# Attention and expert layer: tile 3 transposed in its own step, values behind the next scores, ScalarE and VectorE copies rearranged

## What is computed

```
h  = layernorm(x)
k, v = split((h @ w_kv_down) @ w_kv_up)         # 16 heads of 64
q  = h @ w_q
y  = softmax(causal(q k^T / 8)) v
x  = x + y @ w_out
h  = layernorm(x)
combine = softmax of the top 2 of (h @ Wr), 8 experts
x  = x + sum_e combine_e * 12**-0.5 * (silu(h @ Wg_e) * (h @ Wu_e)) @ Wd_e
```

## Time and profile before

| | |
|---|---|
| median of 3 runs | 951.95 us (951.78 to 955.58) |
| profiled execution | 954.19 us, its span 952.4 us |
| attention steps 1 to 62 | 32.2 to 685.3 us of the span |
| first expert tile | 732.3 us |
| busy over the span | TensorE 94%, VectorE 65%, ScalarE 62%, GpSimd 57% |

### The profile page before, as it was taken

One profiled execution on the slowest core, in us unless ns is written; L12 is line 12 of the kernel. 1 busy time (PEld: TensorE's weight loads), 2 busy tenths in 40 slices (PEclk: granted clock), 3 DMA queues, 4 the chain that ended last, 5 costly groups with the idle time before them and its releaser, 6 DMA issues.

```text
span 952.4 us, 19227 instructions
## 1 busy us (share of the span) xinstructions
PE 898.0 (94%) x5614; PEld 619.5 (65%) x5615; DVE 616.8 (65%) x2378; ACT 585.8 (62%) x1486; POOL 543.1 (57%) x536
## 2 busy tenths in 40 slices
PE   6899999999999999999999999999851999999996
PEld 3566666666666666666666666665531888888885
DVE  3666677777767777776776677677854454455453
ACT  3676777677667766776676677667631555544553
POOL 3555564666466556646655764665553466666555
PEclk9999999999999999999999999999985999999999
DMA  7765410000000000000000000000011233333332
GB/s 201 279 280 225 147 47 1 7 12 18 1 14 19 5 7 12 18 1 13 20 3 7 13 18 1 12 20 4 3 32 34 37 48 47 46 46 44 44 45 28
DMA packets 43991, 44.29 MB, mean 47 GB/s; under 512 B 4352, under 2 KB 35968, under 8 KB 43920
## 3 DMA queue, kind: packets, MB, share of 16 engines
q0 software_dynamic: 16528, 26.03, 11.3%
q1 hardware_dynamic: 27392, 17.39, 6.6%
HBM read 15.28 MB, written 28.12 MB: 46 GB/s over the span
## 4 chain that ended last, share of the span: by engine, by line
PE 91%; issue 4%; DVE 2%; ACT 1%; POOL 1%; SPq 0%; POOLq 0%; DMA 0%; DVEq 0%
PE low_ps L979 15%; PE low_ps L967 9%; PE mid_ps L903 8%; PE low_ps L1130 7%; PE mid_ps L905 6%; PE mid_ps L904 6%; PE out_ps L986 6%; PE mid_ps L946 6%; PE top_ps L946 5%; PE top_ps L967 4%; PE low_ps L946 4%; PE out_ps L1122 4%; PE top_ps L903 2%; PE top_ps L905 2%; PE top_ps L904 2%
## 5 line engine op out<-in xcount | busy, mean ns | idle before, releaser
L328 POOL TENSOR_TENSOR prob<-prob,row_inv 128x512 f32<-128x512 f32 (+3 forms) x256 | 321.3, 1255 | 283.1 <-DVE row_inv L639 281.0
L460 ACT ACTIVATE prob<-prob,neg_max 128x256 f32<-128x256 f32 (+3 forms) x512 | 280.9, 551 | 172.8 <-DVE neg_max L632 172.8
L979 PE MATMUL low_ps<-PT,v_sb 128*64 128x512 f32 (+3 forms) x1024 | 151.9, 439 | 2.4 <-ACT PT L466 2.4
L415 POOL DMA_INDIRECT out<-prob,meta_row x71 | 110.9, 1562 | 35.9 <-issue 34.8
L979 PEld LDWEIGHTS low_ps<-PT,v_sb 128*64 128x64 f32 x1024 | 67.8, 136 | 94.0 <-issue 64.9
L967 PEld LDWEIGHTS low_ps<-ident,prob 128*128 128x128 f32 x768 | 86.4, 140 | 60.1 <-issue 50.9
L967 PE MATMUL low_ps<-ident,prob 128*128 128x128 f32 x768 | 108.3, 277 | 3.1 <-DVE neg_max L632 2.4
L860 DVE TENSOR_TENSOR prob<-mid_ps,prob 128x512 f32<-128x512 f32 x71 | 49.1, 692 | 90.4 <-ACT prob L563 74.1
L460 ACT ACTIVATION_READ_ACCUMULATOR prob<-prob,neg_max 128x1 f32 x512 | 96.7, 189 | 0.0
L632 DVE CUSTOM_DVE_ANT_0 prob<-mid_ps,mask 128x128 f32<-128x128 f32 (+1 forms) x256 | 93.6, 421 | 1.6 <-PE mid_ps L946 0.8
L632 DVE CUSTOM_DVE_ANT_0 prob<-top_ps,mask 128x512 f32<-128x512 f32 x128 | 83.2, 688 | 11.7 <-PE low_ps L967 11.6
(11 more groups left out here) (172 smaller groups left out, 1699.8 us busy)
## 6 DMA issues: line engine op xcount, KB each, us to landing
routed_rows<-W_dn POOLq DMA_DIRECT2D x8, 2080.0 KB
routed<-routed_rows SPq DMA_DIRECT2D x71, 65.0 KB
X<-in_L_attn_x SPq DMA_DIRECT2D x8, 256.0 KB, 5.5
W_ffn<-in_L_ffn_Wg SPq DMA_DIRECT2D x8, 256.0 KB, 5.7
W_ffn<-in_L_ffn_Wu SPq DMA_DIRECT2D x8, 256.0 KB, 6.9
W_dn<-in_L_ffn_Wd SPq DMA_DIRECT2D x8, 256.0 KB, 4.6
out<-X SPq DMA_DIRECT2D x8, 256.0 KB, 2.3
out<-prob,meta_row POOLq DMA_INDIRECT x71
```

Of the source, the lines that this page charges most:

```text
L328: nc.gpsimd.tensor_tensor(p_pair(i), p_pair(i), row_inv[:, i, :].unsqueeze(2).to_broadcast([P, 2, P * (i + 1)]), ALU.mult).then_inc(S["nor ...
L415: nc.gpsimd.indirect_dma_start(out=out, out_offset=bass.IndirectOffsetOnAxis(ap=meta_row[:, q:q + 1], axis=0), in_=eo_sb[q], in_offset=Non ...
L460: nc.scalar.activation(p_at(i, h), p_at(i, h), ACT.Exp, bias=neg_max[:, i, h:h + 1], scale=-1.0, accum_out=row_sum[:, i, h:h + 1]).then_in ...
L979: last = nc.tensor.matmul(y_ps[h * HD:(h + 1) * HD, j * P:T], v_sb[:, half, j, o + h * HD:o + (h + 1) * HD], PT[:, h, j, j:NT, :].rearrang ...
```

## The change

- **TensorE.** Tile 3's transposes move from behind the next step's scores to the end of their own step, and go to `top_ps`; tile 2's go to `low_ps`. A step is now: four scores; `values` of n - 1; `project` for n + 1; transposes of tile 1; batch work; `project_out` of n - 1; transposes of tile 2; `v_chunk` for n + 3; transposes of tile 0; (at k = 4) logits; transposes of tile 3. Before step 1 tile 3 of step 0 is transposed, and the wait for all weights moves from step 1 to the fourth `project`.
- **Waits.** `values` waits for the next step's first maxima; tile 2's transposes for the copy of tile 1's; tile 0's for both copies of q and k; scores of tile 1 for the copy of tile 2's, of tile 3 for the copy of tile 3's.
- **ScalarE.** `qk_copy` becomes two copies of 512 columns, each with its own signal, still in plain fp32; `y_copy` comes over from VectorE. The order is exponentials of tiles 1, 0, (output copy), 2, 3; `y_copy`; `qk_copy`; batch work; weight split; `v_copy`; `t3_copy`.
- **VectorE.** One piece of batch work stands between the reciprocals of tiles 2 and 3, another at the end of a step; the long ones are cut in two (`post_x2` and `post_stats`, `post_aggr`; `post_choose` and `post_chosen`; `post_rows` and `post_weights`). The copies come in the order of tiles 1, 2, 0.
- **GpSimd.** The four multiplications of a step stand together; the scatters follow them, 3 at k = 7, 3 at k = 8, 2 at k = 1. Before the last batch's variance 5 are left beside the 3 of step 63.
- **Weight splits** come at steps 54, 55, 61, 62 and 63 and three at the end.
- **Buffers.** `xn_sb` lies in unused blocks of `PT`, `xn2T` is `outT`, the experts' second `hT` buffer is `y_sb`.

```diff
-            ps, o = {2: (top_ps, 0), 3: (low_ps, 0)}[i]
+            ps = {2: low_ps, 3: top_ps}[i]
@@ GpSimd
             def step(n, k, pre=None, post=None, fills=False):
-                if n:
-                    norm(n - 1, 3)
                 if pre is not None and k == 2:
                     pre_rstd(pre)
-                if post is not None and k == 3:
+                if post is not None and k == 4:
                     post_rstd(post)
-                norm(n, 1)
+                for i in ORDER:
+                    norm(n, i)
                 if fills and k < FILLS:
                     fill(k)
-                norm(n, 0)
-                if post is not None and k in SCATTER_LATE:
-                    scatter_at(post, k, SCATTER_LATE[k])
-                norm(n, 2)
+                if post is not None and k in SCATTERS:
+                    scatter_at(post, k)
@@ ScalarE
             def qk_copy(n):
-                seen(act, S["qk_ready"], n + 1)
-                nc.scalar.activation(qk_sb[:, :, :].rearrange("p a n -> p (a n)"), mid_ps[:, :], ACT.Copy)
+                for a in range(2):
+                    seen(act, S["qk_ready"], 2 * n + a + 1)
+                    nc.scalar.activation(qk_sb[:, a, :], mid_ps[:, a * T:(a + 1) * T], ACT.Copy)
+            def step(n, k, cur=True, nxt=True, pre=None, post=None, v=True):
+                if cur:
+                    exps(n, 1)
+                    exps(n, 0)
                 if post is not None and k == 1:
                     post_out(post)
                 if cur:
-                    exps(n, 1)
-                    exps(n, 0)
-                if prev:
-                    t3_copy(n - 1)
-                if cur:
                     exps(n, 2)
+                    exps(n, 3)
+                y_copy(n - 1)
                 if nxt:
                     qk_copy(n + 1)
...
+                if n in SPLIT_AT:
+                    split_hi(SPLIT_AT[n])
+                if v:
+                    v_copy(n + 3, (k + 3) % NP // NT, (k + 3) % NT)
+                if cur:
+                    t3_copy(n)
@@ VectorE
                     maxes(n, 3)
                     inv(n, 0)
+                    inv(n, 2)
+                if n - 1 in SPLIT_AT and cur:
+                    split_lo(SPLIT_AT[n - 1])
...
                 if cur:
-                    inv(n, 2)
-                if prev:
-                    y_copy(n - 1)
-                if cur:
-                    t_copy(n, 1)
                     inv(n, 3)
+                    t_copy(n, 1)
+                    t_copy(n, 2)
                     t_copy(n, 0)
-                    t_copy(n, 2)
...
@@ TensorE
             def scores(n, i):
                 if i == 1:
-                    seen(pe, S["t1_copied"], n)
+                    seen(pe, S["t2_copied"], n)
...
                 if i == 3:
-                    seen(pe, S["t2_copied"], n)
+                    seen(pe, S["t3_copied"], n)
...
             def transposes(n, i):
                 seen(pe, S["norm_done"], NT * n + POS[i] + 1)
+                if i == 2:
                     seen(pe, S["t1_copied"], n + 1)
                 if i == 0:
+                    seen(pe, S["qk_copied"], 2 * min(n + 2, STEPS))
...
             def values(n, pair, cur):
-                seen(pe, S["t3_copied"], n + 1)
+                if cur:
+                    seen(pe, S["max_done"], 8 * (n + 1) + 2)
...
                 if cur:
                     for i in ORDER:
                         scores(n, i)
-                if prev:
-                    transposes(n - 1, 3, cur)
+                values(n - 1, (k - 1) % NP, cur)
                 if nxt:
                     project(n + 1, (k + 1) % NP, m + (k + 1) // NP)
-                if prev:
-                    values(n - 1, (k - 1) % NP, cur)
-                if v:
-                    v_chunk(n + 3, m + (k + 3) // NP, (k + 3) % NP // NT, (k + 3) % NT)
                 if cur:
                     transposes(n, 1)
...
-                if prev:
-                    project_out(n - 1, (k - 1) % NP)
+                project_out(n - 1, (k - 1) % NP)
+                if cur:
+                    transposes(n, 2)
+                if v:
+                    seen(pe, S["qk_copied"], 2 * n + 3)
+                    v_chunk(n + 3, m + (k + 3) // NP, (k + 3) % NP // NT, (k + 3) % NT)
                 if cur:
                     transposes(n, 0)
-                    transposes(n, 2)
+                if post is not None and k == 4:
+                    post_logits(post)
+                if cur:
+                    transposes(n, 3)
```

More of the change, by code:

```diff
@@ L137, in layer @@
         meta_row = sb("meta_row", [P, RING], I32)
+        xn_sb = [PT[:, 0, j, i, :] for j, i in ((1, 0), (2, 0), (2, 1), (3, 0))]
+        xn2T = outT
         up_hi = Wb[:, :, :]
@@ new lines, in step @@
+                if n - 1 in SPLIT_AT and cur:
+                    split_lo(SPLIT_AT[n - 1])
+                if pre is not None and k == 1:
+                    pre_stats(pre)
+                if post is not None and k == 2:
+                    post_x2(post)
+                if pre is not None and k == 3:
+                    pre_norm(pre)
+                if post is not None and k == 4:
+                    post_xn2(post)
+                if post is not None and k == 5:
+                    post_choose(post)
@@ L675, in step @@
+                if post is not None and k == 7:
+                    post_weights(post)
                 if cur:
-                    inv(n, 2)
-                if prev:
-                    y_copy(n - 1)
+                    inv(n, 3)
+                    t_copy(n, 1)
                 if cur:
-                    t_copy(n, 1)
-                    inv(n, 3)
+                    t_copy(n, 2)
                     t_copy(n, 0)
-                    t_copy(n, 2)
-            def split_weights(k, part=slice(None)):
-                for e in SPLIT_HI[SPLIT_AT.get(k - 1, SPLIT_AT.get(k - 2, 0)):SPLIT_AT[k]][part]:
-                    dve.wait_ge(S["split_hi"], SPLIT_HI.index(e) + 1)
-                    nc.vector.tensor_tensor(up_lo[:, e, :], W_ffn[:, e, :], up_hi[:, e, :].bitcast(F32), ALU.subtract)\
-                        .then_inc(S["split_lo"], 1)
+                if post is not None and k == 2:
+                    post_stats(post)
@@ new lines, in step, with split_lo @@
+                if post is not None and k == 3:
+                    post_aggr(post)
+                if pre is not None and k == 3:
+                    pre_lo(pre)
+                if post is not None and k == 5:
+                    post_chosen(post)
+                if post is not None and k == 6:
+                    post_rows(post)
+            def split_lo(e):
+                dve.wait_ge(S["split_hi"], SPLIT_ORDER.index(e) + 1)
+                nc.vector.tensor_tensor(up_lo[:, e, :], W_ffn[:, e, :], up_hi[:, e, :].bitcast(F32), ALU.subtract)\
+                    .then_inc(S["split_lo"], 1)
@@ L741, in post_rows @@
             def post_rows(b):
-                def made(k):
-                    seen(dve, S["routing"], ROUTING * b + k)
-                def sig(ins):
-                    ins.then_inc(S["routing"], 1)
                 seen(dve, S["ranks_ready"], b + 1)
@@ L772, in _ @@
             dve.wait_ge(S["base_set"], 1)
-            maxes(0, 1)
-            maxes(0, 0)
-            maxes(0, 2)
+            for i in (1, 0, 2):
+                maxes(0, i)
             inv(0, 1)
@@ L782, in _ @@
             w_lo(Wv, 1, 4, post_ps[:, :])
-            t_copy(0, 1)
             inv(0, 3)
-            t_copy(0, 0)
-            t_copy(0, 2)
+            for i in (1, 2, 0):
+                t_copy(0, i)
             w_lo(Wk, 1, 5, post_ps[:, :])
@@ L911, in pre_T @@
                 for t in range(NT):
-                    last = nc.tensor.transpose(xT_ps(b)[:, t * P:(t + 1) * P], xn_sb[:, t, :], ident[:, :])
+                    last = nc.tensor.transpose(xT_ps(b)[:, t * P:(t + 1) * P], xn_sb[t], ident[:, :])
                 last.then_inc(S["xT_ready"], 1)
@@ L970, in values @@
             def values(n, pair, cur):
-                seen(pe, S["t3_copied"], n + 1)
-                for i in range(NT - 1 if not cur else 0):
+                if cur:
+                    seen(pe, S["max_done"], 8 * (n + 1) + 2)
+                for i in range(NT if not cur else 0):
                     seen(pe, S[f"t{i}_copied"], n + 1)
@@ L1077, in _ @@
                 v_chunk(t, 0, 0, t, t % 2)
-            for i in (1, 0, 2):
+            for i in (1, 2, 0):
                 transposes(0, i)
@@ L1081, in _ @@
             fold("k1", post_ps[:, :], T)
+            transposes(0, 3)
             pe.wait_ge(wo_in, 16)
-            pe.wait_ge(S["wlo_done"], 6)
             for k in range(1, NP + 1):
```

149 lines of the change are left out of this document (62 added, 87 removed).

## The result

The changed kernel takes 957.02 us, the median of five runs (956.73 to 957.93), beside 953.95 us (951.78 to 955.58) for the kernel before in the same rounds. The ratio is 1.0037, 95% interval [1.0021, 1.0054]. That is no gain, but a loss of some 3 us, and outside the range of 936.5 to 950.3. How large the loss is stays uncertain: in later rounds the kernel before took 954.36 and 957.20 us in the median, with single executions from 951.7 to 960.3. The distance to the forecast is clear of that. The profiled execution took 956.87 us, its span is 955.1 against 952.4 us, and the forecast for that span was 943.2. So 11.9 us of span have to be found.

The account below looks back on a forecast made before the run. TensorE's own sequence was taken as the bound. Terms -9.5 - 5.4 + 4.8 + 1.5 + 1.0 + 0.9 - 2.5 = -9.2 us took the span from 952.4 to 943.2, or 942.7 us against the median; range 936.5 to 950.3.

Parts of the forecast that it names:

- Part 1: TensorE's new order: three changes of array shape a step instead of four, 0.153 us less, 9.5 us over 62 steps.
- Rival B: TensorE's border from scores to values costs 0.25 us instead of 0.15, giving 948.9 us; chance 0.08.
- Part 2: TensorE's waits for row maxima, made late behind VectorE's batch work, go in steps 1 to 62: 5.4 us gained.
- Part 4: ScalarE takes y and separate q and k copies at no cost; 1.5 us allowed for output-copy or late-VectorE steps.
- Part 3: Tile 2's transposes newly wait for VectorE's copy of tile 1's: 0.14 us in 34 steps, 4.8 us lost.
- the slower rival: ScalarE becomes the bound of the step through a late copy of y: 962.7 us; chance 0.07.
- Part 5, start: Tile 3's transposes of step 0 ahead of step 1, plus a q copy, start step 1 later: 0.9 us lost.
- Part 5, end: After step 63 begins, the last batch's variance comes at 19.5 us instead of 22.0: 2.5 us gained.
- within 0.5%: Whole kernel: time differs from the kernel before by under 0.5% of the median, 4.8 us; chance 0.22.

Follow-up runs that it names:

- experiment 4: The changed kernel with weight splits at the step's end and, in step 0, copies of tiles 1 and 2 ahead of tile 3's reciprocal: 957.08 us.
- experiment 3: The kernel before with only the two normalisations at k = 3 and k = 4 moved behind the reciprocal of tile 2: 962.27 us.

## Why the prediction was wrong

- **Part 1 held.** Three changes of shape instead of four, the border from scores to values at 0.95 us: the undisturbed step came out at 10.19 us as summed (10.00 and a wait of 0.19, where 10.05 and 0.14 were taken). Rival B didn't happen. The step before less the step after plus the wait that came is 10.20 - 10.19 + 0.19 = 0.20 us for the change of shape that went and the overlaps with it. The estimate of 0.053 us from the drain of 128 cycles in the Trainium skill, "TensorE: Matmul & The Clock Gate", section "Step-by-step: what each phase is for", is too small here; the trace's own borders were the better guide.
- **Part 2 held for the most part in its size.** Of the 5.4 us some 4 went: steps 17, 24, 35, 46, 57 and 59 to 61 were longer than others of their kind before (by 0.2 to 1.1 us), and are not any more. Step 62 fell from 11.00 to 10.56 only; the 0.95 left went with the weight split in experiment 4. But its sentence on VectorE's gaps is where part 4's error begins.
- **Part 3 was mis-sized by little**: 0.19 instead of 0.14 us. What I missed is that it is avoidable, and that T1 ahead of the passes saves 0.26 us a step.
- **Part 4 is the step that failed**, in the sentence "In the steps that copy the output or have VectorE late I allow 1.5 us in all", with part 2's "The new order spreads that work into VectorE's gaps". I costed VectorE's batch work by its durations in the kernel before and took the gap behind the reciprocal of tile 2 as free. That reciprocal is what releases GpSimd. The gap of one engine was the busiest place of the other, and the durations didn't carry over: 14 x 0.61 = 8.5 us, against the 1.5 allowed for all such waits. The kernel before showed the effect in a row that I passed over, the normalisations' median of 335 ns beside a longest of 755 (experiment 3). ScalarE, which I watched instead and made the slower rival of, was in time: in steps 1 to 62 y was waited for only in step 1 (0.24 us), though by 1.0 us in step 63, which has no q and k passes.
- **The weight splits** in the same gap cost 2.5 us in steps 55, 56 and 62, by the same mechanism; nothing stood for them in the sum. Step 1 costs 1.05 us over the forecast: VectorE's last weight corrections stand ahead of its maxima (the values wait 0.68 us). That is read from the trace; no run moved them. Against these 12 us stand about 3 us of allowances not used and steps with k = 1 and 4 slightly cheaper than forecast.
- **Part 5, start:** 1.3 us instead of 0.9, and that it is so near is luck. From T1 of step 0 to step 1 it took 7.26 us instead of 5.01, 2.25 more; T1 itself happened to begin 0.95 us earlier (26.22 instead of 27.17). What I had not counted was T2's wait for the copy of T1, 2.53 us, with the fall of the clock behind it.
- **Part 5, end:** I had GpSimd's multiplications of step 63 end at 9.0 us; they ended at 10.0 (697.79), since the split held the one of tile 0 back. One of eight scatters took 1.96 us instead of 0.95 to 1.05, beside a weight split on VectorE, and the step between two is 1.27 us. In all eleven traces every scatter over 1.3 us runs beside such a split. So the variance began at 21.6 us instead of 19.5, and of 2.5 us only 0.4 were gained:

```profile
708.33 0.95 POOL L349 DMA_INDIRECT routed_rows<-routed,row_i  x1 [0.30 <-issue]
709.30 0.22 POOL L339 TENSOR_TENSOR rstd<-mv,eps 128x4 f32<-128x4 f32 x1
```

- **After it** 0.6 to 0.7 us more, which I had costed at nothing. Half of it lies between the first expert tile and tile 10 (28.5 us before, 28.9 after). It is not a later return of the clock, which came 4.7 us after the first tile before and 4.3 after; what it is stays open.
- **The median.** I took the 2.2 us of the profiled execution over the median as time around the span. It is in the span: all executions take 1.7 to 1.8 us more than their spans. The forecast of 942.7 doesn't change by it.

The outcome falls in the case "within 0.5%", which had 0.22, but by none of its mechanisms. Left open is what decides how late the clock returns. In four kernels it came 4.3 to 5.2 us after the first expert tile, and tiles 0 to 10 took 28.5 to 28.9 us; in the seven others it came 8.8 to 10.6 us after it, and they took 30.4 to 30.9, with the same instructions there. Each kernel has one trace, so this can differ between executions of one kernel as well. It is worth up to 2 us, and gains at the end of attention can vanish in it, as in experiment 4. No run was made to find its rule. Nor was T3's new place tried by itself.

## What to carry to other kernels

Before work is moved into an engine's gap, look at what GpSimd and VectorE do at the same time there: here a 0.34 us VectorE instruction became 1.5 us beside GpSimd, and the same four instructions moved ahead of the reciprocal that releases GpSimd cost TensorE no wait. In a group of equal instructions a maximum far above the median can hint at such exclusion before any change is made. When an engine is the bound and waits come singly, they add up: three small moves together took 18.7 us off steps 1 to 62, where the separate runs had given 18.1.

## What the hardware showed that I had not expected

- Some of VectorE's SBUF-to-SBUF instructions and GpSimd's multiplications hold each other up, both ways. A normalisation (`tensor_scalar`) ends 0.08 to 0.10 us behind GpSimd's instruction, whatever is left of it (0.34 us becomes up to 1.51, behind a scatter and a multiplication 2.33); a multiplication of 0.61 us becomes 1.57 behind a subtraction of two SBUF tensors.
- Others are not held up, though they read and write SBUF only. In the kernel after, 16 of the 32 statistics below start well inside a multiplication, and none takes over 294 ns; the reciprocals beside one took 0.17 us where they take 0.14 to 0.17.

```profile
L603 DVE BATCH_NORM_STATS2 stats_a<-X x32: 272/276/294, 4.2 to 544.5; 128x6 f32<-128x128 f32 x32
```

- VectorE's maxima, which read scores from PSUM, ran beside a multiplication in their usual time (two of 0.67 and 0.69 us in step 55, beside the one of tile 1).
- After T2's wait of 2.53 us in step 0 TensorE was at the lower clock (0.60 on average in 28 to 32 us); after one of 0.88 us it stayed at 1.00, and so it did in the kernel before after the 2.15 us ahead of step 1.
